# Causal attention between two feed-forward blocks: units in groups of three, and one row maximum in six taken by ScalarE and GpSimd

## The reference

```
x = x + 0.5 * ffn(layernorm(x))
x = x + attn(layernorm(x))
x = x + 0.5 * ffn(layernorm(x))

Q, K, V = x @ WQ[h], x @ WK[h], x @ WV[h]          # 16 heads, 16 columns each
scores  = where(causal, Q @ K.T / 4, -inf)         # 4096 x 4096 for each head
attn    = sum_h softmax(scores) @ V @ WO[h]
```

## Time and profile before

| | |
|---|---|
| median of 3 runs | 1996.3 us (1994.75 to 1996.97) |
| profiled execution, first to last instruction | 1995.0 us |
| PE busy | 1949.6 us, 98% |
| DVE busy | 1677.5 us, 84% |
| ACT busy | 1355.3 us, 68% |
| POOL busy | 304.6 us, 15% |
| chain that ended last | PE 92%, DVE 4%, ACT 2% |

### The profile page before, as it was taken

One profiled execution on the slowest core, in us unless ns is written; L12 is line 12 of the kernel. 1 busy time (PEld: TensorE's weight loads), 2 busy tenths in 40 slices (PEclk: granted clock), 3 DMA queues, 4 the chain that ended last, 5 costly groups with the idle time before them and its releaser, 6 DMA issues.

```text
span 1995.0 us, 58983 instructions
## 1 busy us (share of the span) xinstructions
PE 1949.6 (98%) x24312; PEld 1198.9 (60%) x24312; DVE 1677.5 (84%) x3630; ACT 1355.3 (68%) x1626; POOL 304.6 (15%) x736
## 2 busy tenths in 40 slices
PE   5999999999999999999999999999999999999999
PEld 3777776555555555555555555555555555569998
DVE  7655566699999999999999999999999999847663
ACT  5312221588888888888888888888888888884444
POOL 2100000011101111111110111111111101134444
PEclk9999999899999999999999999999999999999999
DMA  6111221212111111211111111111122111101110
GB/s 196 51 51 51 74 77 51 74 40 52 40 47 46 44 42 39 53 40 49 45 44 39 44 48 41 50 43 44 41 46 46 39 53 29 60 28 64 59 48 22
DMA packets 82812, 102.20 MB, mean 51 GB/s; under 512 B 16752, under 2 KB 45168, under 8 KB 82544
## 3 DMA queue, kind: packets, MB, share of 16 engines
q1 hardware_dynamic: 81920, 98.03, 17.4%
q10 hardware_dynamic: 624, 0.40, 0.1%
HBM read 68.46 MB, written 29.36 MB: 49 GB/s over the span
## 4 chain that ended last, share of the span: by engine, by line
PE 92%; DVE 4%; ACT 2%; issue 1%; DMA 1%; POOL 0%; SPq 0%; POOLq 0%; ACTq 0%; DVEq 0%
PE PS L1142 33%; PE PS L1269 32%; PE PS L1119 7%; PE PS L1089 6%; PE PS L1249 6%; PE PS L1328 4%; PE PS L1194 2%; PE PS L1113 1%; PE PS L1055 1%; ACT PG L700 1%; DVE BNS L745 1%; DVE OA L798 1%; DMA PG<-w_exp_t 1%; ACT OA L608 1%; POOL QT L577 0%
## 5 line engine op out<-in xcount | busy, mean ns | idle before, releaser
L700 ACT ACTIVATE PG<-PS 128x1024 f32<-128x1024 f32 (+1 forms) x1152 | 1116.0, 977 | 233.8 <-PE PS L1249 173.2
L930 DVE TENSOR_REDUCE MXP<-PS 128x1 f32<-128x512 f32 x1792 | 1099.7, 685 | 20.5 <-PE PS L1142 20.4
L1249 PE MATMUL PS<-QT,KT 50*128 50x512 f32 (+1 forms) x2304 | 802.3, 434 | 0.0
L1142 PE MATMUL PS<-KT,QT 48*128 48x512 f32 (+3 forms) x2304 | 797.1, 431 | 2.6 <-DVE MXP L930 2.3
L1269 PE MATMUL PS<-PG,VH 128*17 128x128 f32 x16896 | 727.5, 276 | 0.4 <-ACT PG L700 0.3
L1269 PEld LDWEIGHTS PS<-PG,VH 128*17 128x17 f32 x16896 | 400.5, 97 | 412.4 <-issue 363.4
L1142 PEld LDWEIGHTS PS<-KT,QT 48*128 48x128 f32 x2304 | 340.2, 185 | 251.8 <-issue 141.9
L1249 PEld LDWEIGHTS PS<-QT,KT 50*128 50x128 f32 x2304 | 335.1, 185 | 10.3 <-issue 9.9
L926 DVE CUSTOM_DVE_ANT_0 PS<-PS,MASK 128x128 f32<-128x128 f32 (+3 forms) x512 | 249.2, 506 | 72.7 <-PE PS L1142 66.9
L557 POOL TENSOR_SCALAR_AFFINE_SELECT PG<-PG 128x128 f32<-128x128 f32 x512 | 136.3, 292 | 995.8 <-ACT PG L700 995.0
L626 ACT ACTIVATE PG<-PS,GB 128x512 f32<-128x512 f32 x128 | 90.3, 706 | 171.3 <-PE PS L1089 171.3
(11 more groups left out here) (110 smaller groups left out, 1197.2 us busy)
## 6 DMA issues: line engine op xcount, KB each, us to landing
QT<-q_parts SPq DMA_DIRECT2D x256, 64.0 KB
KT<-k_parts SPq DMA_DIRECT2D x256, 64.0 KB
q_parts<-OA SPq DMA_DIRECT2D x16, 512.0 KB, 2.8
QT<-q_parts SPq DMA_DIRECT2D x256, 32.0 KB
k_parts<-OA SPq DMA_DIRECT2D x16, 512.0 KB, 4.6
KT<-k_parts SPq DMA_DIRECT2D x256, 32.0 KB
o_parts<-OS SPq DMA_DIRECT2D x128, 64.0 KB
OA<-o_parts SPq DMA_DIRECT2D x32, 256.0 KB
```

What stands on the lines that cost most here:

```text
L700: nc.scalar.activation(PB[n % 2][half][:, :, q0:TILE], PS[:, half * 1024:half * 1024 + 1024].rearrange("p (k q) -> p k q", k=2)[:, :, q0:T ...
L930: nc.vector.tensor_reduce(dst, bank(b), AX.X, ALU.max).then_inc(mx_red, 1)
L1142: mm(bank(4 + qs % 2 if b is None else b, w), q[0:SC, (BT * place(j) + qs) * P:(BT * place(j) + qs + 1) * P].bitcast(f32r), k[0:SC, c * TI ...
L1249: last = mm(PS[:, (2 * half + k) * 512 + q0:(2 * half + k + 1) * 512], kt[0:SM, kb * P:(kb + 1) * P].bitcast(f32r), qt[0:SM, place(j) * TI ...
```

## The change

The key block becomes the unit of the loop: 144 units for a head, 2304 in all. They are issued in groups of three. TensorE's queue for a group is score, maximum, score, maximum, score, maximum, and then the values of the units of the group before (`VALUES_IN`; where a query tile ends inside a group, the values stop there and the next group has more). Each unit has one score bank of three (0 to 2), one buffer of eight for its exponential, and one exponential instruction of at most 512 columns; on the diagonal it has 512, 384, 256 or 128. The freed bank 3 becomes the fourth bank for the maxima. The semaphores that were kept for two halves become one each, counted in units.

Of each head's maxima those at place 4 of every 6, if off the diagonal and but for 70 and 142, are not reduced by VectorE. In the running numbers of the units this is always the third unit of a group with an even number, 292 maxima in all. ScalarE copies the bank to one of six SBUF buffers behind the group's exponentials, which frees the bank (`copy_maxima`); GpSimd folds the 512 columns to 256 by max(a, b) = max(b - a, 0) + a, three dependent instructions (`fold`); VectorE reduces the 256 columns three groups later (`final_maximum`). GpSimd's queue for a group is its masks, then the fold, then V copies. ScalarE's is three exponentials, the copy, and the sums of a tile that ended. The buffers lie where the projections' parts were, so ScalarE waits once, before its first exponential, for the last of their stores. The second output projection's blocks and one transpose are put at group numbers that answer to their former slots. SyncE's loads follow the new counts.

```
-SLOT_N = H * NCH + 1
+UNITS = [(j, c, k) for j, c in CH for k in range(BT)]
+NU = len(UNITS)
+UNIT_N = H * NU
+GROUP = 3
+GROUP_N = UNIT_N // GROUP + 1
+VALUES_BEHIND = 3
+FINAL_BEHIND = 3
+S_BANKS = 3
+P_BUFFERS = 8
+C_BUFFERS = 6
+FOLD_WIDTHS = (256,)
+FOLD_STEPS = 3 * len(FOLD_WIDTHS) - 1
...
+COPIED = frozenset(m for m in range(NU) if m % 6 == 4 and m not in (70, 142))
+WO_AT, XT_AT = (24, 25, 26, 28), 37
...
-MAX_BANKS = (4, 5, 7)
+MAX_BANKS = (4, 5, 7, 3)
...
+        COPY = [oa[:, 5 * DK * TILE + i * TILE:5 * DK * TILE + (i + 1) * TILE] for i in range(C_BUFFERS)]
...
+        COPY = [oa[:, 5 * DK * TILE + i * TILE:5 * DK * TILE + (i + 1) * TILE] for i in range(C_BUFFERS)]
...
+        VALUES_IN, first = [], 0
+        for g in range(GROUP_N):
+            last = min(GROUP * (g + 1) - VALUES_BEHIND, UNIT_N) if g < GROUP_N - 1 else UNIT_N
+            stop = next((u + 1 for u in range(first, last) if ends_tile(u)), last)
+            VALUES_IN.append(range(first, stop))
+            first = stop
...
+        def copied(u):
+            _, _, j, c, _ = unit(max_item(u))
+            return u < MX_UNITS and j != c and max_item(u) % NU in COPIED
+        def items_in(g):
+            return [u for u in group_units(g) if u < MX_UNITS]
+        def finals_in(g):
+            return [u for u in items_in(g - FINAL_BEHIND) if copied(u)] if g >= FINAL_BEHIND else []
+        COPY_N = {u: n for n, u in enumerate(u for u in range(MX_UNITS) if copied(u))}
+        COPIES = list(COPY_N)
+        RED_N = {}
+        for g in range(GROUP_N):
+            for u in finals_in(g) + [u for u in items_in(g) if not copied(u)]:
+                RED_N[u] = MX_AHEAD + FREE_MX + len(RED_N) + 1
...
+            def mask(u):
+                _, _, j, c, kb = unit(u)
+                if j == c:
+                    pool.wait_ge(exp_done, u + 1)
                     pool.sem_inc(passed[0], 1)
-                    for k in range(2):
-
-                        kb = 2 * half + k
-                        tri = PB[n % 2][half][:, k, kb * P:(kb + 1) * P]
-                        nc.gpsimd.affine_select(out=tri, in_=tri, compare_op=ALU.is_ge, fill=0.0, base=0,
-                                                pattern=[[1, P]], channel_multiplier=-1
-                                                ).then_inc(masked[half], 1)
+                    tri = PB[u % P_BUFFERS][:, kb * P:(kb + 1) * P]
+                    nc.gpsimd.affine_select(out=tri, in_=tri, compare_op=ALU.is_ge, fill=0.0, base=0,
+                                            pattern=[[1, P]], channel_multiplier=-1).then_inc(masked, 1)
+            def fold(u):
+                n = COPY_N[u]
+                c = COPY[n % C_BUFFERS]
+                pool.wait_ge(mx_copied, n + 1)
+                steps = FOLD_STEPS * n
+                for k, w in enumerate(FOLD_WIDTHS):
+                    done = steps + 3 * k
+                    d = c[:, w:2 * w]
+                    nc.gpsimd.tensor_tensor(d, d, c[:, 0:w], ALU.subtract).then_inc(fold_step, 1)
+                    pool.wait_ge(fold_step, done + 1)
+                    nc.gpsimd.tensor_scalar(d, d, 0.0, None, ALU.max).then_inc(fold_step, 1)
+                    pool.wait_ge(fold_step, done + 2)
+                    last = nc.gpsimd.tensor_tensor(c[:, 0:w], d, c[:, 0:w], ALU.add)
+                    if w != FOLD_WIDTHS[-1]:
+                        last.then_inc(fold_step, 1)
+                        pool.wait_ge(fold_step, done + 3)
+                last.then_inc(mx_folded, 1)
...
+            for g in range(GROUP_N):
+                for u in group_units(g):
+                    mask(u)
+                for u in items_in(g):
+                    if copied(u):
+                        fold(u)
+                copies_v_in(g)
...
+            for w in range(1, 4):
+                act.wait_ge(parts_out[w], 16 * (NT + 1))
...
+            def exponential(u):
+                _, _, j, c, k = unit(u)
+                q0 = P * k if j == c else 0
+                if u >= P_BUFFERS:
+                    act.wait_ge(pv_done, u - P_BUFFERS + 1)
+                act.wait_ge(st_ps, u + 1)
+                nc.scalar.activation(PB[u % P_BUFFERS][:, q0:TILE], bank(u % S_BANKS)[:, q0:TILE],
+                                     ACT.Exp, scale=1.0 / DH ** 0.5).then_inc(exp_done, 1)
+            def copy_maxima(u):
+                n = COPY_N[u]
+                if n >= C_BUFFERS:
+                    act.wait_ge(mx_red, RED_N[COPIES[n - C_BUFFERS]])
+                act.wait_ge(mx_ps, max_item(u) + 1)
+                nc.scalar.activation(COPY[n % C_BUFFERS], bank(mx_bank(u)), ACT.Copy).then_inc(mx_copied, 1)
...
+            for g in range(GROUP_N):
+                for u in group_units(g):
+                    exponential(u)
+                for u in items_in(g):
+                    if copied(u):
+                        copy_maxima(u)
+                for u in VALUES_IN[g]:
+                    if ends_tile(u):
+                        take_sums(u)
...
+            def final_maximum(u):
+                _, n, j, c, qs = unit(max_item(u))
+                dve.wait_ge(mx_folded, COPY_N[u] + 1)
+                nc.vector.tensor_reduce(MXP[:, BT * place(j) + qs, c:c + 1], COPY[COPY_N[u] % C_BUFFERS][:, 0:FOLD_WIDTHS[-1]],
+                                        AX.X, ALU.max).then_inc(mx_red, 1)
+            for g in range(GROUP_N):
+                for u in finals_in(g):
+                    final_maximum(u)
+                steps = splits_in(g)
+                for u in group_units(g):
+                    if u < MX_UNITS and not copied(u):
+                        _, n, _, _, qs = unit(max_item(u))
+                        maximum(max_item(u), n, qs, mx_bank(u))
+                    for i, k in steps[u % GROUP:u % GROUP + 1]:
+                        split_step(*divmod(i, 2), k)
...
+            def bank_free(u):
+                before = u - len(MAX_BANKS)
...
+                elif u == 2:
+                    pe.wait_ge(v_ev, NT * BT + FREE_V)
+                elif before >= 0 and copied(before):
+                    pe.wait_ge(mx_copied, COPY_N[before] + 1)
+                elif before >= 0:
+                    pe.wait_ge(mx_red, RED_N[before])
...
+                if u >= S_BANKS:
+                    pe.wait_ge(exp_done, u - S_BANKS + 1)
+                kb = c * BT + k
+                kt, qt = (NK, NQ) if alone and u % 2 else (CK, CQ)
+                mm(bank(u % S_BANKS)[:, q0:TILE], kt[0:SM, kb * P:(kb + 1) * P].bitcast(f32r),
+                   qt[0:SM, place(j) * TILE + q0:(place(j) + 1) * TILE].bitcast(f32r),
+                   start=True, stop=True).then_inc(st_ps, 1)
...
+                for qs in range(kb if j == c else 0, BT):
+                    last = mm(O_SUM[qs * Q32:qs * Q32 + DV, :], VH[:, c * BT + kb, :],
+                              PB[u % P_BUFFERS][:, qs * P:(qs + 1) * P],
+                              start=(j == c and kb == 0), stop=(c == 0 and kb == (qs if j == c else BT - 1)))
+                last.then_inc(pv_done, 1)
...
+            for g in range(GROUP_N):
+                for u in group_units(g):
+                    scores(u)
+                    ahead_maximum(u)
...
+                for u in VALUES_IN[g]:
+                    values(u)
+                last_head = g - (H - 1) * NU // GROUP
...
```

More of the change, by code:

```diff
@@ L105, in program @@
         PG = sb("PG", [P, HB, TILE])
-        PB = [[PG[:, 4 * i + 2 * k:4 * i + 2 * k + 2, :] for k in range(2)] for i in range(2)]
+        PB = [PG[:, i, :] for i in range(P_BUFFERS)]
         VH = sb("VH", [P, NB, DV])
@@ L339, in program, with unit, group_units, ends_tile @@
         O_SUM = bank(O_BANK, P)
+        MX_AHEAD = AHEAD * BT
+        MX_UNITS = UNIT_N - MX_AHEAD
+        def unit(u):
+            h, i = divmod(u, NU)
+            return h, i // BT, *UNITS[i]
+        def group_units(g):
+            return range(GROUP * g, min(GROUP * (g + 1), UNIT_N))
+        def ends_tile(u):
+            _, _, _, c, k = unit(u)
+            return c == 0 and k == BT - 1
+        VALUES_IN, first = [], 0
[4 more added lines that the diff above has]
+            first = stop
         def tile_ended(n):
@@ L1238, in scores @@
                         pe.wait_ge(m_ld[g], (h + 1) * 16 * BT)
-                q0 = 2 * P if j == c and half else 0
-                last_slots = h * NCH + n >= H * NCH - AHEAD
-                if half == 0 and h * NCH + n == H * NCH - AHEAD:
+                q0 = P * k if j == c else 0
+                alone = u >= MX_UNITS
+                if u == MX_UNITS:
                     pe.wait_ge(m_ld_n[0], 16 * BT)
-                if half == 0 and last_slots and c == j and j == ORDER[FIRST_ROWS]:
+                if alone and k == 0 and c == j and j == ORDER[FIRST_ROWS]:
@@ L1244, in scores @@
                     pe.wait_ge(m_ld_n[1], 16 * BT)
-                pe.wait_ge(exp_done[half], h * NCH + n + 1)
-                for k in range(2):
```

(17 more changed lines are left out.)

173 lines of the change are left out of this document (53 added, 120 removed).

## The result

The changed kernel takes 2071.8 us (median of 4 runs, 2068.7 to 2076.5) against 1996.5 of the kernel before: a ratio of 1.0378, 95% interval 1.0362 to 1.0394. The forecast was 1998.3 and the range 1930 to 2050, so the time lies outside it, on the slow side. Medians leave out slow executions, of which three of the experiments had one each: with the loads at the split it was the profiled one (3353 us), so that kernel's trace is not used, and its 2019.0 in the expectations is 2018.0 here.

The account below looks back on a forecast made before the run. TensorE was taken to set the pace, VectorE nearly as full. Heads -7 us (87.6 against 88.0 each), start +4 and tail +5 gave +2 on 1995.0, plus 1.3 for the median: 1998.3 us, range 1930 to 2050.

Parts of the forecast that it names:

- rival A: Faster: neither masks nor third score late; masks alone free 1926 us, both free 1880; chance 0.24.
- The failed step: Split steps, next head's loads and V copies keep their places and cost nothing (0 to 0.3 us a head).
- TensorE's new group: TensorE's group of three takes 1.665 us, 0.555 a unit against 0.611; 125 us to gain if nothing takes it.
- ScalarE and three score banks: Third score waits for the third exponential; two groups take 3.52 us, 3.0 us a head over the floor.
- rival C: Slower: exponentials with two waits each do not overlap; two groups take 4.18 us of ScalarE; about 2113 us; chance 0.09.
- Masks behind the fold: GpSimd's 2.06 us fold delays masks; TensorE stalls eight times a head, 4.7 us a head, 72 in all.
- rival B: Slower: GpSimd's one-input operation costs what the two-input one does; sign: fold over 2.3 us; 41 us, 2039; chance 0.17.
- VectorE: Not the pace, so relief alone buys nothing; its 3.25 us per two groups is hidden against 3.52.
- Start: ScalarE's first exponential waits for the last store of the key parts: about +4 us (0 to 5).
- Tail: Last 92 units, without maxima: third score late, 1.70 us for three units against 1.48, +5 us.

Follow-up runs that it names:

- the half fold: Changed kernel with loads at the split, the fold's three operations on 128 columns instead of 256, the others left out of the maximum: 1955.1 us.
- grouping with free relief: Groups of three, loads at the split, no copies, no start wait; VectorE reduces one off-diagonal maximum in six over 256 of 512 columns: 1909.7 us.
- both orders mended: Changed kernel with the loads of the maxima issued at the split and each fold put behind the next group's masks: 1974.3 us.

## Why the prediction was wrong

Three kernels on record lead from the forecast to the result. With loads at the split and the half fold, TensorE stands only 2.7 us in the middle and the time is 1955.1; the full fold ahead of the masks adds 63 (2018.0); the late loads add 54 (2071.8). The forecast had, in the same order, 1926 for the kernel with its masks alone free (rival A), 72 for the masks, 0 for the loads. So it was 29 us too low in the first, 9 too high in the second, and 54 too low in the third. (In the first, masks still delay weight loads, so part of the 29 may be theirs.) That the kernel with loads at the split, 2018.0, lies inside the forecast's own 1975 to 2022 owes something to luck, as the first two errors offset in part.

Prices from different kernels don't add up here: grouping with free relief 1909.7, the start's wait 8.3 and the copies 3.6 would give 1921.6, 33 us under the 1955.1.

- **The failed step** is "Split steps, loads for the next head and V copies keep their places: nothing either, since they had tens of us or TensorE's group to hide in". VectorE's split steps do keep their places. The loads of the split maxima don't: SyncE's list is written in the old slots of a chunk, four units, and the new slot number, (split_group + 2) x 3 / 4, puts them behind waits for score and maximum matmuls of the next chunks. They had no tens of us to hide in: in the kernel before, the load goes out 9.0 us ahead of the score that reads it, and issue and landing take 4.8 (928.14 to 932.93 in the chain above), so some 4 us are spare. The change takes 5.1. In its own shorter way to that score, 7.2 us where the loads go out in time (890.31 to 897.48 with both orders mended), only 2.4 are spare: by this estimate 2.7 us too late, and 2.6 were measured. The other load of a head goes out 1.0 us behind its transpose with 14.5 us to go to its score, and nothing waits for it. The standing once a head, and half the clock for 3 to 14 us behind it, are 54 us here, 83 with the masks in time, and the whole distance between the forecast and the result but for 20. A queue's program order was in the diff, and its price could have been had from the trace: the time from the load to the first score that reads it.
- **TensorE's new group**: right. Groups that wait for nothing are 1.66 to 1.68 us apart, their x24 values blocks take 0.78 (0.77 forecast), their pairs 0.42, 0.23 and 0.23.
- **ScalarE and three score banks**: 3.0 us a head over the floor forecast; with copies, half folds and relief 84.6 - 79.9 = 4.7 are left, without copies 2.2. For two groups without masks 3.52 was forecast and 3.56 is measured, so the size is about right there and the rest lies in groups with masks or behind them; that it is the third score which waits is not shown, since four score banks could only be tried at the price of a maximum bank. Exponentials overlap (without it two groups would take 4.18), so rival C fell.
- **Masks behind the fold**: mechanism right, and two errors that nearly cancel. The one-input operation takes 845 ns where 400 was taken, so the fold is 2.47 us (0.73 + 0.85 + 0.73 and waits), beyond the 2.3 that the prediction named as rival B's sign. By the prediction's own sum that makes 4.7 + 8 x 0.445 = 8.3 us a head. But TensorE waits 78 times in 13 heads, 6 a head of 0.63, not 8: 3.8 us. That 63 us measured come near the 72 forecast is luck in part. Rival B was priced at 2039; the kernel with loads at the split took 2018.
- **VectorE**: "as DVE is not the pace, that alone buys nothing" holds for the kernel before (three reductions 3 x 0.585 = 1.755 against 1.83 for three units). In the shorter group VectorE is the pace, and the relief is worth 30 us when nobody pays for it. In the change ScalarE's copies and GpSimd's folds together cost 79 us with that relief taken off (2018.0 against 1939.4).
- **Start**: +4 forecast, 8.3 measured; the first exponential is at 380.84 in place of 374.68, behind this store:

```profile
375.72 4.96 DMA k_parts<-OA
...
380.84 0.61 ACT PG L777
```

- **Tail**: 1.70 a full group forecast. In the grouping-only kernel the last ones come 1.48 and 1.95 apart in turn, 1.71 in the mean, and the tail of 92 units is 4.2 us longer than before (5 forecast): right.

Open: the kernel with loads and masks both mended is at 86.0 us a head, the one with the half fold at 84.6, and adding up the parts would give 82.3. The first difference is about the 1.3 us of mask waits that are left. The second is not settled: the finals are ruled out, and copies beside a relieved VectorE account for some 1.1 us of it.

## What to carry to other kernels

When a change regroups a loop, every engine's program has to be read again in the new order, the DMA-issuing one above all: for each transfer, take from the trace of before how long after its data is ready it goes out and how soon it is wanted, and see what waits are now ahead of it. A helper engine that is idle most of the time is not free if its queue is in order: here pieces of 2.47 us ahead of urgent ones of 0.29 us cost 63 us more than pieces of 1.6 us; put the urgent ones first, or leave it alone. And judge the parts of a combined change one by one: here the grouping, with its fourth maximum bank, was worth 57 us by itself, and the copies and folds cost more than that. And don't add prices that were measured in different kernels: here their sum was 33 us off.

## What the runs showed of the hardware

- VectorE's reduction of 256 columns takes 409 ns from the copy and 415 ns straight from the bank, against 682 for 512: halving the columns takes away 40% of the time.
